# A 16-head attention block between two quantized FFNs: parts of q and k stored once and loaded in groups, the start rearranged, the last FFN in halves

## The reference

```
x = x + 0.5 * ffn(layernorm(x), w_ffn, b_ffn)
x = x + attn(layernorm(x), Wq, bq, Wk, bk, Wv, bv, Wo, bo, phase, threshold, temperature)
x = x + 0.5 * ffn(layernorm(x), w_ffn, b_ffn)
```

## Time and profile before

| | us |
|---|---|
| median of 3 runs | 971.29 |
| lowest and highest | 967.44, 976.59 |
| the profiled execution | 967.31 |
| its span, first to last instruction | 965.4 |
| TensorE busy in it | 752.2 (78%) |
| ScalarE busy | 682.9 (71%) |
| VectorE busy | 519.1 (54%) |
| GpSimd busy | 178.5 (18%) |
| data moved by DMA | 181.54 MB |

### The profile page before, as it was taken

The page is one execution under the profiler, slowest core; times in us unless marked ns, Lnnn a source line. Parts: engine busy times, 40 slices in busy tenths (PEclk is TensorE's granted clock), DMA queues, the critical chain, the costliest instruction groups (busy, mean ns, idle before and its releaser), DMA issues.

```text
span 965.4 us, 12701 instructions
## 1 busy us (share of the span) xinstructions
PE 752.2 (78%) x4355; PEld 259.3 (27%) x4355; DVE 519.1 (54%) x1275; ACT 682.9 (71%) x823; POOL 178.5 (18%) x154
## 2 busy tenths in 40 slices
PE   0355942489998788999987989999789888998943
PEld 0031320023222221334322323333223222322323
DVE  8732433467454237656785376566754322565364
ACT  1387753388886687888875888887667888888810
POOL 0201642010333202003344020033350000020010
PEclk9985555599999899999998999999999999999986
DMA  6316586945576766554766766547577665464201
GB/s 167 65 77 271 202 323 231 326 146 157 171 248 222 247 213 194 180 178 155 237 220 216 245 211 185 167 166 225 179 258 245 203 194 167 148 199 127 100 8 47
DMA packets 78120, 181.54 MB, mean 188 GB/s; under 512 B 17712, under 2 KB 42320, under 8 KB 67920
## 3 DMA queue, kind: packets, MB, share of 16 engines
q1 hardware_dynamic: 78048, 180.64, 57.5%
HBM read 115.51 MB, written 65.11 MB: 187 GB/s over the span
## 4 chain that ended last, share of the span: by engine, by line
PE 45%; DVE 15%; ACT 11%; SPq 10%; DMA 10%; issue 8%; POOL 1%; DVEq 0%; POOLq 0%; ACTq 0%
PE S_PS L1393 17%; PE O_PS L1406 15%; DVE S_PS L1088 6%; ACT BIG L650 6%; DMA BIG<-shift_rows 5%; SPq L321 5%; PE F_PS L1303 3%; PE R_PS L1415 3%; PE S_PS L1570 2%; ACT BIG L695 2%; SPq L308 2%; PE P_PS L1303 1%; DMA BIG<-ln_masks 1%; DMA BIG<-in_L_attn_x 1%; PE F_PS L1298 1%
## 5 line engine op out<-in xcount | busy, mean ns | idle before, releaser
L650 ACT ACTIVATE BIG<-S_PS 128x1024 f32<-128x1024 f32 x512 | 508.4, 1023 | 168.0 <-PE S_PS L1393 166.3
L1393 PE MATMUL S_PS<-BIG 98*128 98x512 bf16 x1024 | 308.6, 395 | 95.6 <-DVE S_PS L1088 58.4
L1406 PE MATMUL O_PS<-BIG,VX 128*9 128x512 f32 x2048 | 273.3, 607 | 0.9 <-issue 0.9
L1088 DVE COPY S_PS<-BIG 128x1024 f32<-128x1024 f32 x128 | 152.1, 1224 | 151.8 <-ACT BIG L650 126.2
L1393 PEld LDWEIGHTS S_PS<-BIG 98*128 98x128 bf16 x1024 | 75.0, 99 | 362.7 <-ACT BIG L650 131.3
L518 POOL TENSOR_TENSOR XDT<-PART 128x512 bf16<-128x512 f32 x32 | 36.0, 1125 | 321.7 <-ACT PART L624 321.6
L1100 DVE RECIPROCAL RD<-R_PS 128x16 f32<-128x16 f32 x64 | 16.4, 257 | 127.3 <-PE R_PS L1415 126.8
L1406 PEld LDWEIGHTS O_PS<-BIG,VX 128*9 128x9 f32 x2048 | 30.9, 88 | 114.6 <-issue 99.3
L495 POOL TENSOR_TENSOR BIG<-BIG,BFH 128x512 f32<-128x512 f32 x16 | 21.9, 1399 | 210.2 <-DVE BIG L957 132.8
L495 POOL TENSOR_TENSOR X<-X,BFH 128x512 f32<-128x512 f32 x16 | 21.8, 1392 | 143.6 <-DVE BIG L957 73.1
L527 POOL TENSOR_TENSOR PART<-PART 128x512 f32<-128x512 f32 x32 | 37.0, 1157 | 60.0 <-DVE PART L1023 58.7
(11 more groups left out here) (162 smaller groups left out, 740.2 us busy)
## 6 DMA issues: line engine op xcount, KB each, us to landing
BIG<-ln_masks SPq DMA_DIRECT2D x62, 1024.0 KB, 6.6
BIG<-q_parts SPq DMA_DIRECT2D x64, 384.0 KB
BIG<-k_parts SPq DMA_DIRECT2D x64, 288.0 KB
ln_masks<-BIG SPq DMA_DIRECT2D x16, 1024.0 KB, 6.2
q_parts<-PART SPq DMA_DIRECT2D x12, 768.0 KB, 3.6
k_parts<-PART SPq DMA_DIRECT2D x24, 384.0 KB, 4.6
q_parts<-PART SPq DMA_DIRECT2D x12, 512.0 KB, 4.5
k_parts<-PART SPq DMA_DIRECT2D x24, 256.0 KB, 3.9
```

What stands on the lines that cost most here:

```text
L650: act.activation(E[:, h % 2, j, 2 * pair:2 * pair + 2, :], S_PS[:, pair, :, :], ACT.Exp, scale=LOG_WEIGHT)\
L1088: ve.tensor_copy(S_PS[:, pair, :, :], LNM[:, h % 2, 2 * pair:2 * pair + 2, :]).then_inc(s["seeded"], 1)
L1393: mm = pe.matmul(S_PS[:, pair, i, :], KT[0:ALL_ROWS, slot, K_COL[j], 128 * kb:128 * kb + 128], QT[0:ALL_ROWS, slot, j, :], start=False, st ...
L1406: mm = pe.matmul(O_PS[32 * j:32 * j + HD + 1, :], VX[:, slot_of(n), j, kb, h, :], E[:, h % 2, j, kb, :], start=kb == 0, stop=kb == T - 1)
```

## The change

- **Parts stored once.** DRAM holds three parts of q and of k, each even and odd, in place of twelve terms: [3][2][128][batch][512]. `store_q` is one DMA for a batch, `store_k` one for a column. k's parts lie in the other order (low, middle, high).
- **Groups of products loaded as rows.** The six products are three groups: parts (0,1,2) of q against (low, middle, high) of k; (0,1) against (middle, high); 0 against high. `load_stack` issues six DMAs: for each group one for k and one for q, of 48, 32 and 16 rows. The functions of the mask are treated alike: a store for q (SyncE) and one for k (ScalarE's queue), then six loads from each of the two queues, and each half of the tiles waits for its own.
- **The start.** VectorE takes from ScalarE the copies of group 0's PSUM tiles, and from GpSimd its squares; TensorE runs batch 0's chain between tiles 17 and 18. GpSimd adds the first bias after the block scales are made. Bounds of the first four batches are made at once (`first_bounds_*`, `BOUND4`), and VectorE copies the turned rows. The x of group 1 goes before the q and k stores of group 0; the order and places of the masks and the order of the heads (`HEAD_ORDER`) change too.
- **Last FFN in halves.** For the last group centre, maxima, rstd, scales, quantize and dequantize run on two batches at a time; the first centre and maxima stand behind the second `add_attention`.

The attention's lists of the groups otherwise stay as they are. Parts of the path that is taken only if a flag finds a large bound change too; it does not run on these inputs. The core of the diff:

```diff
+GROUPS = ((0, 3), (3, 5), (5, 6))
+HEAD_ORDER = [0, 8, 1, 2, 3, 4, 5, 6, 7, 9, 10, 11, 12, 13, 14, 15]
-        Q_D = nc.dram_tensor("q_parts", [2, 2 * len(TERMS), 128, QB, L], BF16).ap()
-        K_D = nc.dram_tensor("k_parts", [2, 2 * len(TERMS), 128, K_COLS, L], BF16).ap()
+        Q_D = nc.dram_tensor("q_parts", [2, 3, 2, 128, QB, L], BF16).ap()
+        K_D = nc.dram_tensor("k_parts", [2, 3, 2, 128, K_COLS, L], BF16).ap()
+        def calls_of(n, k):
+            return 2 if k == 1 or (k == 2 and n == NQ - 1) else 1
             def store_q(n, j):
-                for part in range(3):
-                    a, b, c = Q_ROWS[part]
-                    src = QPN[:, part, 0:ns, :].rearrange("p s l -> p (s l)")
-                    sp.dma_start(dst[:, a:b:c, :],
-                                 src[:, None, :].to_broadcast((128, len(range(a, b, c)), ns * L)))\
-                      .then_inc(s["parts_out_q"], 16)
+                sp.dma_start(Q_D[slot_of(n), :, j % 2, :, j:j + ns, :].rearrange("a p s l -> p a (s l)"),
+                             QPN[:, :, 0:ns, :].rearrange("p a s l -> p a (s l)")).then_inc(s["parts_out_q"], 16)
             def store_k(n, j):
                 for col in K_COLS_OF[j]:
-                    for part in range(3):
-                        a, b, c = K_ROWS[part]
-                        sp.dma_start(dst[:, a:b:c, :],
-                                     KP[:, part, None, :].to_broadcast((128, len(range(a, b, c)), L)))\
-                          .then_inc(s["parts_out_k"], 16)
+                    sp.dma_start(K_D[slot_of(n), :, j % 2, :, col, :].rearrange("a p l -> p a l"), KP[:, :, :])\
+                      .then_inc(s["parts_out_k"], 16)
             def load_stack(m):
-                sp.dma_start(KT[0:QK_ROWS, slot, 0:K_COLS, :].rearrange("p c l -> p (c l)"),
-                             K_D[n % 2, :, rows].rearrange("a d c l -> a d (c l)")).then_inc(s[f"stack_in{slot}"], 16)
-                sp.dma_start(QT[0:QK_ROWS, slot, :, :].rearrange("p c l -> p (c l)"),
-                             Q_D[n % 2, :, rows].rearrange("a d c l -> a d (c l)")).then_inc(s[f"stack_in{slot}"], 16)
+                for a, b in GROUPS:
+                    rows = slice(PART_ROWS * a, PART_ROWS * b)
+                    sp.dma_start(KT[rows, slot, 0:K_COLS, :].rearrange("p c l -> p (c l)"),
+                                 K_D[slot_of(n), 3 - (b - a):3, :, head, :, :].rearrange("a e d c l -> (a e) d (c l)"))\
+                      .then_inc(s[f"stack_in{slot}"], 16)
+                    sp.dma_start(QT[rows, slot, :, :].rearrange("p c l -> p (c l)"),
+                                 Q_D[slot_of(n), 0:b - a, :, head, :, :].rearrange("a e d c l -> (a e) d (c l)"))\
+                      .then_inc(s[f"stack_in{slot}"], 16)
...
             for h in MASK_ORDER[0:8]:
                 store_mask(h)
+            lnm_stored(sp, 3)
+            load_x(1)
             for j in range(QB):
                 store_q(0, j)
                 store_k(0, j)
...
             load_stack(0)
+            sp.wait_ge(s["bound_copied"], QB)
+            for e in range(2):
+                for j in (e, e + 2):
+                    ns = 1 if j == QB - 1 else 2
+                    sp.dma_start(SHIFT_D[0, e, j:j + ns, :, :].rearrange("s h (t l) -> (h t) s l", t=T),
+                                 CB4[:, j, 0:ns, :]).then_inc(s["bound_out"], 16)
+            for h in range(11, 13):
+                store_mask(h)
             load_shift(0)
...
+            grid(0)
+            for e in (0, 2):
+                first_xd_copy(e)
+                first_xd_copy(e + 1)
+                add_ffn(0, 0, e)
+                add_ffn(0, 0, e + 1)
+                stats1(0, e)
+                stats1(0, e + 1)
             for e in range(2):
                 rstd(0, 1, e)
                 norm(0, 2 * e)
                 norm(0, 2 * e + 1)
+            first_xnt(0)
+            for j in range(QB):
+                first_full(j, "q")
+                first_square(j, "q")
+                hi_part(0, j, "q")
+                first_full(j, "k")
+                mid_part(0, j, "q")
+                first_square(j, "k")
+                hi_part(0, j, "k")
+                v_part(0, j)
+                if j + 1 < QB:
+                    first_xnt(j + 1)
+                mid_part(0, j, "k")
+                negative(0, j)
+                k_top(0, j)
+            first_bounds_sq()
+            first_bounds_rows()
+            first_bounds_copy()
             seed(0, 0)
             seed(0, 1)
...
             def epilogue(n):
                 for j in range(QB):
                     add_attention(n, j)
+                    if j == 1 and calls_of(n, 2) == 2:
+                        centre(n, 1, 0)
+                        block_tops(n, 1, 0)
+                for e in range(calls_of(n, 2)):
+                    if e == calls_of(n, 2) - 1:
+                        centre(n, 1, e)
+                        block_tops(n, 1, e)
+                    rstd(n, 2, e)
+                    block_scales(n, 1, e)
+                    to_grid(n, 1, e)
+                    from_grid(n, 1, e)
                 for j in range(QB):
                     add_ffn(n, 1, j)
```

More of the change, by code:

```diff
@@ L39 @@
 K_COLS = 3
-BATCH_OF = (0, 2, 1, 3)
+K_COLS_OF = ((0,), (0, 1), (1, 2), (2,))
+K_STORES = 16 * sum(len(c) for c in K_COLS_OF)
+K_LOADS = 16 * (2 * len(GROUPS) + 1)
 CH = 128 // NH
@@ L156, in macaron_kernel @@
         KP = PART[:, 6144:7680].rearrange("p (a l) -> p a l", a=3)
+        Q_PARTS = [QPN[:, a, 0, :] for a in range(3)]
+        K_PARTS = [KP[:, 2 - a, :] for a in range(3)]
         SQR = XDT[0][:, :].bitcast(BF16).rearrange("p (i l) -> p i l", i=2)
@@ L235, in slot_of, with calls_before @@
             return n % 2 if is_short(n) else 0
+        def calls_of(n, k):
+            return 2 if k == 1 or (k == 2 and n == NQ - 1) else 1
+        def calls_before(n, k):
+            return sum(calls_of(i, k) for i in range(n))
         def epilogue_bank(n, j):
@@ L636, in bound_copy @@
                 act.wait_ge(s["bound_turned"], g + 1)
-                if past(g) and is_short(n):
-                    act.wait_ge(s["bound_out"], 16 * g)
+                act.wait_ge(s["bound_out"], 16 * g)
                 for i, scale in ((0, 1.0), (1, -1.0)):
@@ L892, in _ @@
             ve.wait_ge(s["trig_v"], n_.n)
-            for F_, P_ in ((FQ, FQP), (FK, FKP)):
-                for part in range(3):
+            for F_, P_, order, name in ((FQ, FQP, (0, 1, 2), "trig_q"), (FK, FKP, (2, 1, 0), "trig_k")):
+                for i, part in enumerate(order):
                     n_(ve.tensor_copy(P_[:, part, :, :], F_[:, :, :]))
-                    if part < 2:
+                    if i < 2:
                         n_(TT(F_[:, :, :], F_[:, :, :], P_[:, part, :, :], ALU.subtract))
-            ve.sem_inc(s["trig_funcs"], 1)
+                ve.sem_inc(s[name], 1)
             for j in range(QB):
@@ L1204, in first_half @@
                 from_grid(n, 0)
-                for j in range(QB):
-                    add_ffn(n, 0, j)
-                    stats1(n, j)
             def parts(n, j):
@@ L1231, in general @@
                     stats0(n, j)
-                first_half(n)
+                grid(n)
+                for j in range(QB):
+                    add_ffn(n, 0, j)
+                    stats1(n, j)
                 for e in range(2):
@@ L1380, in turn_bound, with turn_first_bounds @@
                           start=True, stop=True).then_inc(s["bound_turned"], 1)
+            def turn_first_bounds():
+                pe.wait_ge(s["bound_row"], 3)
+                for j in range(QB):
+                    pe.matmul(R_PS[0:NH * T, 128 * j:128 * j + 128], BROW4[:, j].rearrange("p h t -> p (h t)"),
+                              IDB[:, :], start=True, stop=True).then_inc(s["bound_turned"], 1)
             def scores(m, k):
@@ L1574, in _ @@
             pe.wait_ge(s["w_grid"], 15)
-            pe.wait_ge(s["trig_in"], 16 * 4)
+            pe.wait_ge(s["trig_in0"], 96)
             for t in range(HALF_TILES):
                 val(t)
-                if t in (7, 11):
-                    j = (t - 7) // 2
+                if t in (10, 13):
+                    j = 0 if t == 10 else 2
                     turn_xd0(0, j)
                     turn_xd0(0, j + 1)
-                if t in (9, 13):
-                    j = (t - 9) // 2
+                if t in (11, 14):
+                    j = 0 if t == 11 else 2
                     ffn0(0, j)
                     ffn0(0, j + 1)
-            chain = {0: (turn_xn, 0), 2: (project_q, 0), 4: (project_k, 0), 6: (project_v, 0), 7: (turn_xn, 1),
-                     8: (norms_k, 0), 9: (project_q, 1), 10: (norms_q, 0), 11: (project_k, 1), 13: (project_v, 1),
-                     14: (turn_xn, 2), 15: (norms_k, 1)}
-            for t in range(HALF_TILES, 2 * HALF_TILES):
+            pe.wait_ge(s["trig_in1"], 96)
+            val(HALF_TILES)
```

(17 more changed lines are left out.)

549 lines of the change are left out of this document (271 added, 278 removed).

## The result

| | before | after |
|---|---|---|
| median, same chips, 4 runs each | 973.94 us (967.44 to 978.11) | 989.6 us (986.32 to 992.7) |
| profiled execution / span | 967.3 / 965.4 us | 986.32 / 984.4 us |
| first copy of a head (ScalarE, L659, now L676) | 197.21 us | 178.39 us |
| from the first copy to the last | 724.7 us | 764.8 us |
| from the last copy to the end of the span | 43.5 us | 41.2 us |

The ratio is 1.0166, 95% interval 1.0095 to 1.0238: slower by 1.7%, where 937 us was forecast. Each split is of one profiled execution. Executions of before lie up to 17.6 us apart over all runs here (965.97 to 983.52), and those of after, e4 and e9 by 6 to 12, so a few us between the heads of these aren't told by one split.

A forecast was written before the change was run, and what follows sets the result against it. No single engine was taken to bound quiet heads, but a once-a-head cycle of exp, seed and scores; start and store-head stalls stood outside. 967.3 - 31 + 5 - 6 - 2.5 = 932.8 profiled, so 937 us median; range 908 to 982.

The forecast's parts named there:

- I take 22 GB/s, 10.3 us: Ordinary heads: the busiest DMA engine works 10.3 us a head, lifting 18 shortest heads by 0.3 each, +5 us.
- 12 us of room: Ordinary heads: a stack asked for at 393.65 is needed a head later, at 405.6, so its landing has 12 us.
- Rival 1: The two lowest DMA engines become the bound in every head: 937 + 109 - 5 = 1041 us; chance 0.14.
- six engines or fewer would not be held back: Stack loads: with 207 GB/s for streams 512 KiB apart, loads on few engines would cost nothing.
- Store heads, -6: 12 heads that store q and k parts: shorter stalls, -6 us in all, ends -30 and +15.
- Rival 3: Store stalls vanish with SyncE's shorter issue and the clock rises in the start: 937 - 20 - 8 = 909; chance 0.15.
- a stall shortens by 0 to 2 us, no more: Heads with stores: fewer stored bytes and issues, set against six loads and a fuller busiest engine, save 0 to 2 us each.
- about 3.9 (to 4.3): Heads with stores: the busiest engine's stack part before the change, in us, growing to 7.8 us after.
- Start, -31: Start up to head 1: first scores near 140, head 1's exps at 155 to 156; -31 us, ends -20 and -42.
- are not ready before 78, so nothing is lost: Start: SyncE's wait for mask 3's store (landed near 77) before x's load costs batch 0's q store nothing.
- Last FFN, -2.5: End: halves shorten the 9 us tail after the last dequantize to about 5.5; -2.5 us, ends -5 and +1.
- SyncE, "no bound": Ordinary heads: SyncE's issues go from 2.5 to 5.6 us of a 10 us head, beside other work no bound.

The follow-up runs named there:

- e4: The kernel before with a head's two stack loads split into six, the eight rows of a part outermost (8 DMA engines): 985.27 us, 1.0138 of before.
- e9: The kernel before with its own two stack loads, the eight rows of a term outermost (8 DMA engines): 980.93 us, 1.0058 of before.
- e2: The kernel after with even and odd copy of a row adjacent in DRAM, so each stack load uses 16 DMA engines: 913.06 us, 0.9386 of before.
- e1: The kernel after with the eight rows of a part outermost in the six stack loads (8 DMA engines): 919.08 us, 0.9426 of before.
- e10: The kernel after with only the one-part group's two loads spread over eight DMA engines (126 KB on the fullest): 941.66 us, 0.9683 of before.
- e3: The kernel before with a head's two stack loads split into six, terms outermost (sizes 6, 4, 2): 1067.27 us, 1.0985 of before.
- e12: e2 with each q and k store made a second time into DRAM that nothing reads: 955.6 us, 0.9799 of before.
- e5: The kernel after with group 1's x load behind batch 0's q and k stores: 988.55 us, 1.0133 of before.
- e6: e2 with group 1's x load behind batch 0's q and k stores: 908.65 us, 0.9313 of before.

## Why the prediction was wrong

By its own sum, profiled 932.8 against 986.3, the miss is 53.5 us: 41.1 in the heads, 12.2 in the start, 0.2 in the end.

**The step that failed: "I take 22 GB/s, 10.3 us ... That lifts only the shortest heads ... +5 us."** The reading before it was right: outer sizes 6, 4 and 2, two engines with 168 KB, and both rates (26 GB/s for the two alone, 17.7 in company). The price was not, for two reasons that the traces show. A rate between the ends was picked by nearness, and the engine's work was held against the head's length. But what decides is the time from the first issue to the last landing, against the room. The same paragraph had worked out 12 us of room, and the traces show 9.8 to 13.8. With 4.3 us of issuing ahead of it, the last load lands in 8.7 us, behind the six others on the two fullest engines: 13.0. And behind the stall of 3.3 us TensorE runs at half clock, 1.6 us more, which the sum had nowhere. Against e2, the same kernel with 16 engines, the narrow loads cost 67.4 us of heads and 7.6 of the start. Rival 1 had the mechanism and priced it at 109; it got 0.14. Its own condition, "about 11.6 us a head, 19 GB/s", was met by the 17.7 of 364 to 370, and not by the 20.6 of 603 to 606. That the run came out within 16 us of before is no merit of the sum: 67 us were lost to the loads while the stores gave far more than the 6 forecast.

The rule of the Trainium skill that was cited (DMA: Bandwidth & Descriptors, Why a DMA increments its semaphore by 16 and not by 1) is borne out by e1, e2 and e10, and on the kernel before by e3 and e4: loads whose outer size was made 8 or 16 lose most of the stall, the share of a stack load rises from 0.33 to 0.53 with outer size 8, and the tail of 0.13 shows two engines. The conclusion drawn beside it from the same page's 207 GB/s (section Latency and other measured facts), that six engines or fewer would not be held back, is not: the sum over all engines was 209 GB/s at 364 to 370 and 54 GB/s in the tail, so it bounds no single engine.

**Store heads, -6.** The bounds (-30 to +15) held the truth and the value taken did not. Storing each part once takes 36.6 us out of the heads (e12), and with the loads on 16 engines the heads are 27.3 us shorter than before. Rival 3, that these stalls vanish, was thus the better description of the stores; in after the two full engines stood in its place. Whether by its reason, SyncE's shorter issue, or by the bytes stays open. The term "a stall shortens by 0 to 2 us, no more" undersized it: a head with twice the stores is up to 7.6 us longer (19.1 against 11.5). Of its parts, "about 3.9 (to 4.3)" us for 56 KB has no row behind it; at 17.8 GB/s from the earlier trace rows they are 3.2.

**Start, -31.** It gained 18.8 to the first copy. The step that failed is that the q store's parts "are not ready before 78, so nothing is lost": the parts were ready at 79.8, mask 3 landed at 80.92 and not 77, and behind x's 1 MB the q store landed in 9.07 us. Without it (e5) the second sigmoids end at 112.00, as forecast (112). The other part is head 1's stack: its landing, 11.87 us in e5 and 6.33 with 16 engines (e6). There head 1's exps begin at 155.61, for a forecast of 155 to 156, and head 0 scores at 141.81 (140). With both faults out, the start is the one that was worked out: the first copy comes 32.2 us earlier than before.

**Last FFN, -2.5.** 2.3 in this pair, 1.7 over all kernels: right.

**SyncE, "no bound".** Right for quiet heads in the main (e1 and e2 issue as much as after). But in after the issues are the first third of a late load, and a cost of the six loads by themselves (e4 against e9, 6.2 us) is neither shown nor excluded.

## What to carry to other kernels

When a load is split or re-shaped, write down the outer size of both sides and from it the kilobytes on the fullest DMA engine; a mean DMA share of 0.5 over the span hid two engines that TensorE waited for 39 times. A load over all engines that lands much later behind its issue, as the mask's here (11.4 us for 6.6), is a sign of it. Then hold first issue to last landing, not busy time, against the room the load has. Here the order of an access pattern was worth 62 us of span (e1) to 74 (e2), and turned a change that is 1.7% slower than before into one that is 6% faster; it is free where the rows are summed over, since a sum doesn't care in which order they lie.

## What was not expected of the hardware

Below the threshold, fewer bytes on the fullest engine still paid: 6.0 us between the medians of e1 and e2, from 84 to 42 KB, with no run of e1 as fast as any of e2 (the 8.8 us of heads are from e1's slowest execution), though quiet heads were hardly late at 84 (the last block, which has no stores, takes 151.8 us in e1 and 150.2 in e2; 161.1 in after). Most of the gain is in the blocks with stores. Two engines that work alone on what is left of loads move 26 GB/s each, an engine in a stack load with no mask beside it 20.6 (e1), and 17.7 at 364 to 370, with masks in flight. The number of busy engines does not explain this by itself: in the earlier trace rows all 16 move 26 GB/s each on the mask stores. And SyncE's own issue of a load takes 0.6 to 0.8 us in a head, but up to 1.40 behind three masks' stores in the start (e6). That a full queue holds the issuer there is likely, but no run tests it.
